# A relu pass as causal mask in a state space mixer, and rings of three score banks with split maxima on GpSimd in an attention

## What is computed

```python
# mixer: 128 heads of 64 in 8 groups, chunks of 128 tokens
A_cum = cumsum(dt * A)                       # per head, within a chunk
L = exp(segsum(A_dt))                        # exp(A_cum[l] - A_cum[s]), 0 above the diagonal
Y_diag = einsum('bzlhn,bzshn,bhzls,bzshp->bzlhp', Cc, Bc, L, xch)
# attention: 32 heads of 16, T = 1024
scores = einsum('bhqd,bhkd->bhqk', q, k) / sqrt(16)
attn = softmax(where(causal, scores, -inf))
y = einsum('bhqk,bhkd->bhqd', attn, v)
```

## Time and profile before

| what | value |
|---|---|
| median of 3 runs | 3235.74 us (3235.0 to 3238.88) |
| the profiled execution's own time | 3237.73 us |
| its span | 3235.9 us |
| busy over the span: PE, DVE, ACT, POOL | 91%, 63%, 32%, 20% |
| mixer, some 130 to 2347 us | 2217 us |
| attention over the heads, 2667 to 3045 us | 378 us |

### The profile page before, as it was taken

How to read it: one execution, slowest core, us unless ns; L and a number is a source line. 1 busy time by engine, 2 the same in 40 slices (tenths; PEclk the granted TensorE clock), 3 DMA queues, 4 the chain that set the end, 5 groups by cost and what they waited for, 6 DMA issues and landing times. The chain is left out here.

```text
span 3235.9 us, 41691 instructions
## 1 busy us (share of the span) xinstructions
PE 2954.3 (91%) x12832; PEld 1668.3 (52%) x12832; DVE 2040.1 (63%) x3246; ACT 1035.7 (32%) x2401; POOL 654.9 (20%) x438
## 2 busy tenths in 40 slices
PE   3799999999999999999999999999879978888889
PEld 2455555555555555555555555555468443333478
DVE  5666666666666676666666676675364647777464
ACT  1233233233233233233333232232221325666421
POOL 1222132222212222221221222222121000000021
PEclk7899999999999999999999999999989888999989
DMA  4001010010001001001010100100010420111000
GB/s 164 15 2 37 1 56 24 14 56 14 23 13 45 24 13 56 15 23 55 2 35 4 56 25 13 55 1 2 10 60 0 164 75 30 37 37 34 6 7 20
DMA packets 55890, 106.97 MB, mean 33 GB/s; under 512 B 24385, under 2 KB 27537, under 8 KB 53009
## 3 DMA queue, kind: packets, MB, share of 16 engines
q1 hardware_dynamic: 50384, 102.60, 9.4%
q10 hardware_dynamic: 5312, 2.00, 0.3%
HBM read 85.71 MB, written 18.87 MB: 32 GB/s over the span
## 5 line engine op out<-in xcount | busy, mean ns | idle before, releaser
L443 PE MATMUL bank<-xnT,wh 128*128 128x512 f32 x1280 | 571.7, 598 | 60.7 <-DVE sg L832 30.0
L587 PE MATMUL bank<-wo,ggT 128*128 128x512 f32 x1024 | 469.5, 613 | 20.2 <-ACT ggT L697 20.2
L535 PE MATMUL bank<-wg,xnT 128*128 128x512 f32 x1024 | 462.2, 594 | 0.0
L443 PEld LDWEIGHTS bank<-xnT,wh 128*128 128x128 f32 x1280 | 236.4, 191 | 332.3 <-issue 290.4
L739 DVE SCALAR_TENSOR_TENSOR cacc<-raw,cwh,cacc 128x512 f32<-128x512 f32 x480 | 390.3, 813 | 17.0
L587 PEld LDWEIGHTS bank<-wo,ggT 128*128 128x128 f32 x1024 | 199.9, 197 | 271.6 <-issue 271.6
L535 PEld LDWEIGHTS bank<-wg,xnT 128*128 128x128 f32 x1024 | 185.1, 191 | 184.5 <-issue 184.5
L510 PEld LDWEIGHTS bank<-xch,em 128*128 128x128 f32 x2048 | 237.4, 194 | 53.6 <-issue 52.0
L915 POOL TENSOR_TENSOR yt<-yt,hd 128x1024 f32<-128x1024 f32 x64 | 153.2, 2394 | 471.9 <-DVE yt L804 407.6
L510 PE MATMUL bank<-xch,em 128*128 128x64 f32 x2048 | 243.5, 278 | 5.1 <-DVE em L781 1.1
L645 ACT COPY xs<-bank 128x512 f32<-128x512 f32 x128 | 74.5, 582 | 522.4 <-PE bank L469 522.4
(11 more groups left out here) (240 smaller groups left out, 4476.2 us busy)
## 6 DMA issues: line engine op xcount, KB each, us to landing
wh<-w_hs_dram SPq DMA_DIRECT2D x80, 256.0 KB, 3.0
wg<-w_gate_dram SPq DMA_DIRECT2D x8, 2048.0 KB, 7.8
wo<-w_out_dram SPq DMA_DIRECT2D x8, 2048.0 KB, 8.0
qk_scratch<-at_part SPq DMA_DIRECT2D x48, 256.0 KB
at_qT<-qk_scratch SPq DMA_DIRECT2D x32, 192.0 KB, 2.6
at_kT<-qk_scratch SPq DMA_DIRECT2D x32, 192.0 KB, 2.6
wgu<-w_gu_dram SPq DMA_DIRECT2D x1, 3584.0 KB, 11.2
at_wa<-w_attn_dram SPq DMA_DIRECT2D x1, 3072.0 KB, 10.4
```

The source lines that it names most:

```text
L443: mm = nc.tensor.matmul(BA[bank][:, :], wh[:, j, k, :], xnT[:, k, h * HALF:(h + 1) * HALF], start=(k == 0), stop=(k == KC - 1))
L535: mm = nc.tensor.matmul(BA[b][:, :], xnT[:, k, ttok], wg[:, k, u * 512:(u + 1) * 512], start=(k == 0), stop=(k == KC - 1))
L587: mm = nc.tensor.matmul(BA[b][:, :], ggT[:, j, :], wo[:, j, :], start=(j == 0), stop=(j == JT - 1))
```

## The change

The mixer loses `negq`, its load and the matmul L481. ACT instead makes relu(-x) of each quarter out of PSUM, which clamps differences above zero, and then exp(-x) in place in SBUF; the causal zeros come from `BC`, whose score half DVE now multiplies by `mask` while copying. `ac_mn` counts the first pass, and pe_diff waits for that; ACT makes the first pass of both quarters before the second pass. In the attention both score rings have three banks with a signal per piece, the maxima `nm` and `nr` are double buffered, the four split operations after the minimum go to GpSimd, and `m_rows` (and ACT's `m_row`) stand after i = 2.

```diff
         def pe_diff(pe, g, z, quarters):
...
             for q in quarters:
-                ac_ex.wait(pe, 4 * n + q - 1)
-                nc.tensor.matmul(BD[q % 2][:, :], identb[:, :], negq[:, :], start=True, stop=False)
+                ac_mn.wait(pe, 4 * n + q - 1)
                 for i in range(QH):
                     hh = slice((q * QH + i) * P, (q * QH + i + 1) * P)
                     mm = nc.tensor.matmul(BD[q % 2][:, i * P:(i + 1) * P], RW[:, 0, hh], RW[:, 1, hh],
-                                          start=False, stop=(i == QH - 1))
+                                          start=True, stop=True)
...
                 pe_df.wait(act, 4 * n + q + 1)
-                nc.scalar.activation(em[:, q, :], BD[q % 2][:, :], ACT.Exp).then_inc(ac_ex.sem, 1)
+                nc.scalar.activation(em[:, q, :], BD[q % 2][:, :], ACT.Relu, scale=-1.0).then_inc(ac_mn.sem, 1)
+            for q in quarters:
+                ac_mn.wait(act, 4 * n + q + 1)
+                nc.scalar.activation(em[:, q, :], em[:, q, :], ACT.Exp, scale=-1.0).then_inc(ac_ex.sem, 1)
...
-            nc.vector.tensor_copy(BC[:, z % 2, :], sm[:, 0:2 * P]).then_inc(dv_sm.sem, 1)
+            nc.vector.tensor_copy(BC[:, z % 2, P:], sm[:, P:2 * P]).then_inc(dv_sm.sem, 1)
+            nc.vector.tensor_tensor(BC[:, z % 2, 0:P], sm[:, 0:P], mask[:, :], ALU.mult).then_inc(dv_sm.sem, 1)
...
-            BST = [BANK[0:2], BANK[2:4]]
-            BS = BANK[4:6]
+            BST, BS = BANK[0:3], BANK[3:6]
...
+                    def split(h, k):
+                        k %= 2
+                        v_mx.wait(pool, MX * (h + 1))
+                        t_m.wait(pool, h)
+                        part = lambda i: mz[:, :, SK + i]
+                        nc.gpsimd.tensor_tensor(part(0), nm[:, k, :], one[:, :], ALU.mult).then_inc(po_mp.sem, 1)
+                        po_mp.wait(pool, 4 * h + 1)
+                        nc.gpsimd.tensor_tensor(nr[:, k, :], nm[:, k, :], part(0), ALU.subtract).then_inc(po_mp.sem, 1)
+                        po_mp.wait(pool, 4 * h + 2)
+                        nc.gpsimd.tensor_tensor(part(1), nr[:, k, :], one[:, :], ALU.mult).then_inc(po_mp.sem, 1)
+                        po_mp.wait(pool, 4 * h + 3)
+                        nc.gpsimd.tensor_tensor(part(2), nr[:, k, :], part(1), ALU.subtract).then_inc(po_mp.sem, 1)
...
+                    def body(h, k):
+                        take(h, k)
+                        if not isinstance(h, int) or h < AH - 2:
+                            split(h + 2, k)
...
-                            v_mx.wait(pe, S1_FROM[NT] * h + m - 1)
+                            v_mx.wait(pe, MX * h + m - (2 if m >= 3 else 3))
...
-                        a_ex.wait(pe, NT * h + j - 1)
-                        for c0_, n, b_ in pieces(j * P, T):
+                        for m, (c0_, n, b_) in enumerate(pieces(j * P, T), S2_FROM[j]):
+                            a_ex.wait(pe, NS_ * h + m - 2)
...
-                            if i == 1 and (not known or h < AH - 1):
+                            if i == 2 and (not known or h < AH - 1):
                                 m_rows(h + 1)
...
-                        t_m.wait(dve, h)
-                        nc.vector.tensor_tensor(nm[:, half:], nm[:, half:], nr[:, half:], ALU.min).then_inc(v_mp.sem, 1)
...
+                        nc.vector.tensor_tensor(nm[:, k, half:], nm[:, k, half:], nr[:, k, half:], ALU.min).then_inc(v_mx.sem, 1)
```

More of the change, by code:

```diff
@@ L454, in pe_pre @@
             ac_xs.wait(pe, 2 * n)
-            dv_sm.wait(pe, n)
+            dv_sm.wait(pe, 2 * n)
             tok = slice(c * P, (c + 1) * P)
@@ L466, in pe_hidden @@
             if u == 1:
-                dv_sm.wait(pe, n + 1)
+                dv_sm.wait(pe, 2 * n + 2)
             for i in range(4):
@@ L776, in dv_masked @@
             n = 8 * g + z
-            dv_sm.wait(dve, n + 1)
+            dv_sm.wait(dve, 2 * n + 2)
             for q in range(NQ):
@@ L1038, in prologue @@
                     ac_exps(act, 0, 0, range(NQ))
-                run(act, ac_slot, prologue, (ac_tail, ac_raw, ac_th, ac_xs, ac_ex, ac_tg, ac_sq, ac_yT))
+                run(act, ac_slot, prologue, (ac_tail, ac_raw, ac_th, ac_xs, ac_mn, ac_ex, ac_tg, ac_sq, ac_yT))
             @block.vector
@@ L1728, in attention @@
             S1_FROM = [sum(len(pieces(0, (k + 1) * P)) for k in range(i)) for i in range(NT + 1)]
-            assert S1_FROM[NT] % 2 == 0
+            NS_ = S1_FROM[NT]
+            MX = NS_ + 1
+            S2_FROM = [sum(len(pieces(k * P, T)) for k in range(j)) for j in range(NT + 1)]
+            assert NS_ % 3 == 0 and S2_FROM[NT] == NS_
             with nc.Block() as block:
@@ L1777, in take, with first @@
                             .then_inc(po_v.sem, 1)
-                    heads(pool, None, take, take, (po_v,))
+                    def split(h, k):
[10 more added lines that the diff above has]
+                        nc.gpsimd.tensor_tensor(part(2), nr[:, k, :], part(1), ALU.subtract).then_inc(po_mp.sem, 1)
+                    def first():
+                        split(0, 0)
+                        split(1, 1)
+                    def body(h, k):
+                        take(h, k)
+                        if not isinstance(h, int) or h < AH - 2:
+                            split(h + 2, k)
+                    heads(pool, first, body, body, (po_v, po_mp))
                 @block.tensor
@@ L1888, in exps @@
                         for j, n in PJ:
-                            t_st.wait(act, NT * h + j + 1)
-                            for c0_, m_, b_ in pieces(0, n):
-                                o = nc.scalar.activation(PT_[:, k % 2, OFF[j] + c0_:OFF[j] + c0_ + m_], BST[j % 2][b_][:, 0:m_],
-                                                         ACT.Exp, scale=SC)
-                            o.then_inc(a_ex.sem, 1)
-                            if j == 1 and (not isinstance(h, int) or h < AH - 1):
+                            for m, (c0_, m_, b_) in enumerate(pieces(0, n), S2_FROM[j]):
+                                t_st.wait(act, NS_ * h + m + 1)
+                                nc.scalar.activation(PT_[:, k % 2, OFF[j] + c0_:OFF[j] + c0_ + m_], BST[m % 3][:, 0:m_],
+                                                     ACT.Exp, scale=SC).then_inc(a_ex.sem, 1)
+                            if j == 2 and (not isinstance(h, int) or h < AH - 1):
                                 m_row(h + 1, k + 1)
@@ L1918, in _, with maxima @@
                 def _(dve):
-                    def maxima(h, between=None):
-                        v_mp.wait(dve, 5 * h)
+                    def maxima(h, k, between=None):
+                        k %= 2
+                        po_mp.wait(dve, 4 * (h - 1))
                         for i in range(NT):
@@ L1957, in first @@
                     def first():
-                        maxima(0)
-                        maxima(1)
+                        maxima(0, 0)
+                        maxima(1, 1)
                     def body(h, k):
@@ L1964, in body @@
                         else:
-                            maxima(h + 2, h - 2 if not isinstance(h, int) or h >= 2 else None)
+                            maxima(h + 2, k, h - 2 if not isinstance(h, int) or h >= 2 else None)
                     def last(h, k):
@@ L1971, in _ @@
                     dve.wait_ge(s_set, 2)
-                    heads(dve, first, body, last, (v_mx, v_mp, v_y, v_ri))
+                    heads(dve, first, body, last, (v_mx, v_y, v_ri))
         with ExitStack() as c2:
```

55 lines of the change are left out of this document (21 added, 34 removed).

## The result

| | before | after |
|---|---|---|
| median | 3237.27 us (3235.0 to 3238.88, 4 runs) | 3202.53 us (3199.63 to 3202.88, 4 runs) |
| profiled execution, span | 3235.9 us | 3200.6 us |
| mixer, start of the first product of `xch` and `em` (L510, now L506) to that of the last slot | 2174.8 us | 2164.1 us |
| attention, one head in the steady part | 11.39 us | 10.78 us |

The ratio is 0.9891, with a 95% interval of 0.9874 to 0.9908: 35 us faster, where 40 were forecast. The time lies inside the range. I read the stages first again.

What follows compares the result with a forecast made beforehand. PE bounds the mixer, the chain between engines the attention heads. Mixer 19 us (12.6 + 12.6 - 5.2 - 1) plus attention 21 us is 40 off 3237.7, shown as 3196 us; range 3178 to 3226.

Steps and rivals of the forecast that it cites:

- Mixer, slots with tiles: Mask matmul gone: 0.42 us kept in each of 30 three-tile slots, 0.84 in each of 15 four-tile slots, 12.6 us each.
- Mixer, z = 7: Seven empty mixer slots: ACT's additional passes (0.64 us) and the `BC` product (0.1) delay PE, 5.2 us lost.
- Kept: nothing: Empty mixer slots of z = 3 and last group: PE waits for the gated output anyway, so removing matmuls gains nothing.
- The 1 us of the prologue: Mixer prologue: four first passes precede the first exponential, 2 us at most less 0.84 on PE; 1 us taken as lost.
- Attention, m_rows: Attention head: `m_rows` moved behind i = 2 lets work ahead of the value products run while PE would wait, gaining 0.70 us.
- Attention, third bank: Attention head: PE makes s1(6)'s first piece ahead of its wait for the reduction of i = 5, gaining 0.33 us.
- Attention, split: Attention head: split on GpSimd makes the chain from minimum to PE 1.53 us instead of 1.19, losing 0.33 us.
- Rival 1: Attention: GpSimd's short operations take 0.50 us, period 11.8 us, 13 us lost, time 3230 us; chance 0.11.
- rival 3: Attention: each split operation on GpSimd costs 0.82 us, period 13.1 us, 51 us lost, time 3268 us; chance 0.07.
- Attention, the sum: Attention: 0.70 us gained a head, period 10.7 us, 21 us over 30 heads.
- Rival 2: Mixer gains only 6 us: `BC` product held or delaying (8 us), ACT's z = 7 passes costing double (5 us), 3209 us; chance 0.13.

Runs made afterwards that it cites:

- the order of ScalarE alone: Changed kernel, at z = 7 ACT's second passes of quarters 0 and 1 placed behind the two scaled copies: 3193.86 us, ratio 0.987.
- this half alone: Kernel before with only the mixer's part of the change: 3226.44 us, ratio 0.9968.
- The doubled matmuls: Changed kernel, with each quarter's difference matmuls made twice in the mixer's empty slots, same result: 3189.93 us, ratio 0.9857.
- the attention's half alone: Kernel before with only the attention's part of the change: 3215.7 us, ratio 0.9931.
- one move: Changed kernel, DVE's output moved from between the reductions of i = 4 and i = 5 to behind the minimum: 3193.17 us, ratio 0.9863.
- the other: Changed kernel, `m_rows` moved behind the first value products and the transposes of the output a column later: 3206.33 us, ratio 0.9906.
- both gave 22: Changed kernel with DVE's output behind the minimum, and `m_rows` and the transposes of the output later: 3180.73 us, ratio 0.983.

## Why the prediction was right, and where it was off

- **Mixer, slots with tiles.** Right. 0.43 and 0.86 us were kept, against 0.42 and 0.84, because what PE occupies was read from distances of starts and not from the 384 ns of a row. The other 0.42 us of a three-tile slot went into the wait, 1.44 us against 1.42.
- **Mixer, z = 7.** Right as a mechanism and in size: 0.67 us against 0.74, and the order of ScalarE alone undoes it.
- **Mixer, "Kept: nothing" in the empty slots.** This is the step that failed. Nothing was kept, but something was lost: 4.5 us at z = 3, 2.9 in the last group and 3.2 at z = 7, 10.6 us in all. The step treated a longer wait of PE as free when nothing else moves. The trace showed the risk: the windows of the mixer had a clock of 0.99, not 1.00, and slots of z = 3 lasted from 28.65 to 31.72 us. Less this loss, the 20 us forecast for the slots (12.6 + 12.6 - 5.2) are 9.4, beside 10.7 by the trace and 10.5 for this half alone. The doubled matmuls show that it is the clock, and that it hangs on PE's work ahead of the waits: ACT's second passes stay in that run, and it is 12.6 us faster. The 1 us of the prologue can't be told: the first product of `xch` and `em` starts from 139.3 to 142.2 us in the traces, 141.3 in that of before.
- **Attention, m_rows.** 0.62 us against 0.70.
- **Attention, third bank.** 0.34 against 0.33, measured with s2 given its fourth bank back, which the term didn't name. I had taken the middle between nothing and 0.67 for lack of a row, and nothing here shows that this was more than luck; the half of two pieces was the argument.
- **Attention, split.** The chain is 1.51 us against 1.53, 0.32 us longer than on VectorE. The row that it rested on, GpSimd's one column add of 0.22 us, was the right one. An operation on 8 columns lasts 0.20 to 0.23 us. Rival 1's 0.50 us and rival 3's 0.82 us didn't occur. My reason for the choice, that DVE doesn't work on SBUF meanwhile, wasn't what decided: in the runs with the output behind the minimum it does, and the four operations still take 205 to 235 ns on average. The estimate by the ratio that the Trainium skill gives (GPSIMD Engine Reference, section 3.1), named beside rival 1, was 0.35 us an operation; the trace shows 0.23 us, and the measurement decides.
- **Attention, the sum.** The steady heads gain 0.61 us, not 0.70, which is 18 us over 30 heads. That the 21.2 us measured equal the forecast is luck: the first three intervals between `m_rows`, counted at nothing, gained 3.8 us with the attention's half alone (31.0 to 27.2 us).
- **The total.** 35 us against 40 misses by less than the mixer's half does, which gave 10.5 us where 19 were forecast. The halves sum to 31.7 us; 3 us of the 34.7 belong to neither, and lie within the intervals.
- **Rival 2**, with 6 us for the mixer, was nearer to the mixer's size than its mechanisms deserve: neither the product into `BC` (281 ns, and tile slots gained all) nor ACT's passes were slower than I took them (a relu pass out of PSUM lasts 607 ns, as the exponential's did).

## What to carry to other kernels

Removing work from PE just ahead of a wait is not free when it comes out of a stretch that is already loose: look at the granted clock of the matmuls behind the wait, in both kernels and in the same part of the loop. A term of an attention loop is worth what it takes of the loop's period, even where no engine shows a wait for it; add up the loop, don't read the idle column alone. When a move helps by less than it takes out of the loop, look for the next thing that is late and move that with it: here one move gave 9 us, the other lost 4, and both gave 22.

## What the runs showed of the hardware that I had not expected

In the empty slots the clock fell though no wait was longer than 1.82 us. With waits of 0.84, 1.75 and 0.68 us in one slot of z = 3, 16 projections took 9.63 us at a granted clock of 0.84 over the window; in the same slot with 16 more difference matmuls, they took 7.10 at 1.00, with waits of 0.40, 1.52 and 1.14 us. More matmuls made the kernel 12.6 us faster. But the lengths of the waits alone don't tell what happens: with 0.41, 1.53 and 1.14 us in the kernel before, the clock fell in five slots of z = 3 (10.11 us for 16 projections in one) and stayed in two (7.11 us). The Trainium skill, TensorE: Matmul & The Clock Gate, section "HAM oscillation — how this bites in real kernels", describes such falls where the engine waits between bursts of matmuls; the traces agree in kind alone. The section speaks of transfers that are waited for, once in each round of a loop, and of longer waits; here the falls come with short waits for other engines, in a kernel whose PE is busy for 91% of its span. And equal slots of one execution differ, 30.14 to 31.37 us in the changed kernel.

A ScalarE pass over 512 columns in place in SBUF (the exponential) lasts 647 ns against 607 for the relu from PSUM, and two of them 1.16 us against 1.09, so the second pass cost hardly more than the first.

GpSimd makes an operation on 8 columns in 0.20 to 0.23 us, and the next that depends on it starts 0.28 to 0.31 us behind it; on DVE the same are 0.17 to 0.20 and 0.21 to 0.23 us.
